# Causal mask of the transposed scores: from a TensorE matmul to GpSimd selects on the exponentials

## The reference

```python
q = (hidden_states @ q_w.T + q_b).reshape(b, s, H, HEAD_DIM)
k = hidden_states @ k_w.T + k_b
v = hidden_states @ v_w.T + v_b
scores = jnp.einsum('bqhd,bkd->bhqk', q, k) / HEAD_DIM ** 0.5
causal = jnp.triu(jnp.ones((s, s), dtype=bool), k=1)
scores = jnp.where(causal[None, None], -jnp.inf, scores)
attn = jax.nn.softmax(scores.astype(jnp.float32), axis=-1).astype(q.dtype)
out = jnp.einsum('bhqk,bkd->bqhd', attn, v).reshape(b, s, H * HEAD_DIM)
return out @ o_w.T + o_b
```

## Time and profile before

| | us |
|---|---|
| median of three runs | 2301.51 |
| lowest and highest | 2300.06, 2307.46 |
| span of the profiled execution | 2299.0 |
| TensorE busy in it | 2144.2 |
| VectorE busy | 1156.6 |
| ScalarE busy | 730.3 |
| GpSimd busy | 473.0 |

### The profile page before, as it was taken

The page is one execution under the profiler, slowest core; times in us unless marked ns, Lnnn a source line. Parts: engine busy times, 40 slices in busy tenths (PEclk is TensorE's granted clock), DMA queues, the critical chain, the costliest instruction groups (busy, mean ns, idle before and its releaser), DMA issues. The chain is left out here.

```text
span 2299.0 us, 33530 instructions
## 1 busy us (share of the span) xinstructions
PE 2144.2 (93%) x11910; PEld 1650.0 (72%) x11910; DVE 1156.6 (50%) x2233; ACT 730.3 (32%) x1273; POOL 473.0 (21%) x851
## 2 busy tenths in 40 slices
PE   6999999999999827999999999999999999999995
PEld 4666676666766516777777777778888888888884
DVE  4666857668576655444444444444424334334232
ACT  3434435344353322444333333332111111111111
POOL 2222414224142212111111111000120220220213
PEclk9999999999999956999999999999999999999998
DMA  6045141451413122444444444333120220210202
GB/s 170 30 108 146 60 131 52 116 140 63 132 49 101 56 74 93 149 148 154 158 158 164 169 161 147 131 110 114 38 91 18 73 91 18 73 61 31 90 19 92
DMA packets 106894, 228.78 MB, mean 100 GB/s; under 512 B 9664, under 2 KB 23744, under 8 KB 103648
## 3 DMA queue, kind: packets, MB, share of 16 engines
q1 hardware_dynamic: 94368, 187.28, 25.3%
q0 software_dynamic: 12480, 40.90, 5.9%
HBM read 160.52 MB, written 66.06 MB: 99 GB/s over the span
## 5 line engine op out<-in xcount | busy, mean ns | idle before, releaser
L1041 PE MATMUL ex_bank<-ex_xT,ex_gu 128*128 128x512 f32 (+1 forms) x1656 | 391.8, 395 | 1.5 <-DVE ex_xT L1075 1.5
L1041 PEld LDWEIGHTS ex_bank<-ex_xT,ex_gu 128*128 128x128 f32 (+1 forms) x1656 | 297.7, 180 | 87.8 <-issue 1.9
L1091 DVE TENSOR_TENSOR sh_silu<-sh_silu,sh_bank 128x512 f32<-128x512 f32 x88 | 60.5, 688 | 444.7 <-ACT sh_silu L1084 401.3
L740 ACT ACTIVATE at_PT<-at_bank 128x512 f32<-128x512 f32 (+1 forms) x384 | 187.4, 526 | 264.6 <-PE at_bank L446 258.3
L590 DVE TENSOR_REDUCE at_nmax<-at_bank 128x1 f32<-128x384 f32 (+3 forms) x512 | 216.7, 472 | 107.1 <-PE at_bank L394 107.1
L1041 PE MATMUL sh_bank<-sh_xT,sh_gate 128*128 128x512 f32 x1056 | 256.2, 392 | 4.1 <-DVE sh_xT L1075 4.1
L1053 PE MATMUL sh_bank<-sh_dn,sh_act 128*128 128x512 f32 x1056 | 255.2, 391 | 0.0
L1041 PE MATMUL sh_bank<-sh_xT,sh_up 128*128 128x512 f32 x1056 | 254.0, 389 | 0.0
L1084 ACT ACTIVATE sh_silu<-sh_bank 128x512 f32<-128x512 f32 x88 | 52.6, 598 | 586.6 <-PE sh_bank L1041 533.6
L800 POOL TENSOR_TENSOR at_minus_max<-idf,at_nmax 128x512 fp32r<-128x512 f32 x128 | 133.7, 1044 | 506.4 <-DVE at_nmax L590 488.0
L1041 PEld LDWEIGHTS sh_bank<-sh_xT,sh_gate 128*128 128x128 f32 x1056 | 199.7, 189 | 46.0 <-DVE sh_xT L1075 4.3
(11 more groups left out here) (207 smaller groups left out, 2882.0 us busy)
## 6 DMA issues: line engine op xcount, KB each, us to landing
ex_gu_in<-gu_in SPq DMA_DIRECT2D x23, 1408.0 KB
at_Qs<-q_dram SPq DMA_DIRECT2D x96, 256.0 KB, 5.8
ys<-sh_yk SPq DMA_DIRECT2D x23, 1024.0 KB, 5.8
q_dram<-at_q_h SPq DMA_DIRECT2D x64, 256.0 KB, 4.3
ex_dn_in<-dn_in SPq DMA_DIRECT2D x23, 512.0 KB
at_x_in<-x_in SPq DMA_DIRECT2D x8, 1024.0 KB, 10.1
at_x_res<-x_in SPq DMA_DIRECT2D x8, 1024.0 KB, 6.3
x<-at_y SPq DMA_DIRECT2D x8, 1024.0 KB, 8.1
```

The lines of the kernel that those rows point to most:

```text
L740: nc.scalar.activation(PT[g % 2][:, h % HG, TFROM[tb]:TFROM[tb] + TW[tb]], T_ps[tb][:, 0:TW[tb]], ACT.Exp).then_inc(pt_ready, 1)
L1041: last = self.nc.tensor.matmul(self.gate_up_ps[c % 2][which][0:m, :], cols(i, k), self.xT[j][:, k, :], start=(step == 0), stop=(step == 3 ...
L1091: nc.vector.tensor_tensor(silu[c % 2][0:m, :], silu[c % 2][0:m, :], gate_up_ps[c % 2][1][0:m, :], ALU.mult).then_inc(s["product"], 1)
```

## The change

The mask matmul of the transposed scores is removed, so that the exponentials of the diagonal blocks hold values for queries earlier than the key too. After the exponentials GpSimd replaces those by zero. A new function, drop_later_queries(b, h), waits for the three units of head h and runs two affine_select on PT in place: one over three of the diagonal blocks (at columns 0, 512 and 1024, evenly spaced), one over the fourth (at column 640). The second signals a new semaphore, pt_masked. Both products over keys now follow a wait for pt_masked in place of pt_ready.

```diff
@@ -413,7 +414,7 @@
                     if s in AV_STEP:
                         g = AV_STEP.index(s)
-                        pe.wait_ge(pt_ready, 3 * H * b + 3 * HG * (g + 1))
+                        pe.wait_ge(pt_masked, H * b + HG * (g + 1))
@@ -439,8 +440,6 @@
-                            nc.tensor.matmul(T_ps[tb][:, 0:len(tiles) * P], mask[:, 0, :],
-                                             idb[:, 0:len(tiles), :].rearrange("p t k -> p (t k)"), start=False, stop=False)
@@ -453,7 +452,7 @@
-                pe.wait_ge(pt_ready, 3 * H * b + 3 * H)
+                pe.wait_ge(pt_masked, H * b + H)
@@ -790,6 +789,18 @@
+            def drop_later_queries(b, h):
+
+                pool.wait_ge(pt_ready, 3 * h + 3)
+                pool.wait_ge(pt_ready, 3 * H * b + 3 * h + 3)
+                pt = PT[(h // HG) % 2][:, h % HG, :]
+                spread = pt.rearrange("p (t k) -> p t k", k=P)[:, 0:QT * QT // 2 + 1:QT, :]
+                nc.gpsimd.affine_select(out=spread, in_=spread, compare_op=ALU.is_ge, fill=0.0, base=0,
+                                        pattern=[[0, QT - 1], [1, P]], channel_multiplier=-1)
+                nc.gpsimd.affine_select(out=pt[:, TOFF[1]:TOFF[1] + P], in_=pt[:, TOFF[1]:TOFF[1] + P],
+                                        compare_op=ALU.is_ge, fill=0.0, base=0, pattern=[[1, P]],
+                                        channel_multiplier=-1).then_inc(pt_masked, 1)
@@ -800,12 +811,15 @@
+                    if h > 0:
+                        drop_later_queries(b, h - 1)
                     if h == 5 and not first:
                         norm[1].refine(b - 1)
                     if h == 8 and not last:
                         norm[0].refine(b + 1)
                     if 8 <= h < 8 + QT and not first:
                         add_residual(b - 1, h - 8)
+                drop_later_queries(b, H - 1)
```

More of the change, by code:

```diff
@@ L213, in build_attention @@
         x1_ready, diagonal_ready, made = sem("x1_ready"), sem("diagonal_ready"), sem("made")
+        pt_masked = sem("pt_masked")
         S_UNITS = [((2, 0), (0, (QT - 1) * P)), ((3, 0),), ((1, 0),)]
```

## The result

| | us, median (range) | runs |
|---|---|---|
| before | 2302.24 (2300.06 to 2307.46) | 4 |
| after | 2338.23 (2332.76 to 2339.73) | 4 |
| ratio after / before | 1.016 (95%: 1.0142 to 1.0178) | |

The changed kernel is slower by 36.0 us. The forecast was +17.5: the sign is right and the time lies in the range of 2290 to 2345, but the loss is twice what the sum gave. The profiled executions differ by 38.9 us of span (2337.9 against 2299.0), so they can be used to look for it.

A forecast was written before the change was run, and what follows sets the result against it. TensorE was taken as the bound, with the loop through VectorE's maxima and GpSimd's minus_max nearly closed. Span 2299.0 + 17.2 (6 x 2.4 + 0.3 + 2.5) + 2.5 around the span = 2319 us; range 2290 to 2345.

The forecast's parts named there:

- the sum: Attention stage: six steady turns at +2.4, first turn +0.3, last turn +2.5, together 17.2 us slower.
- T without a wait: Transposed part of a head's scores on TensorE: 1.70 us with three masks, 1.40 without, 0.30 saved a head.
- the MEMSET slope: Low bound for GpSimd's 384-column select: 0.8 ns a column, giving 0.49 us; 0.53 was taken.
- the residual add: High bound for the 384-column select: a two-input GpSimd operation, 1.275 us for 512 columns, so 0.96.
- the rival with the dear select: GpSimd's 384-column select goes at the two-input add's pace, a drop of 1.3 us: 22 us more, 2341; 8%.
- the three groups named: Groups 0 to 2, steps 5, 9, 13: TensorE's product over keys waits for selects, 1.3 to 1.7 us each.
- the fourth group's: Its product stands behind 60 products of the next sequence's projections, so its drop is hidden, except in the last turn.
- The gain lands in part only: Of 38 us gross, plain steps gain little: 0.6 by head 5's scores, then 0.3 for each of seven heads.
- the step-by-step working: Shifts through a steady turn: products of groups 0, 1, 2 at +0.7, +1.6, +3.0, turn's end at +2.4 us.
- at full granted clock: Reading of a steady turn before the change: TensorE busy 94.0 of 96.4 us at full clock.
- VectorE and GpSimd hold each other up: Rival: three hits of 0.5 us a turn on VectorE's path to the maxima add 12 us, 2331; 9%.
- 0.3 for the first turn: No residual adds and no chain at head 5 there: three waits against seven gains, about +0.3 us.

The follow-up runs named there:

- the kernel with the low halves later: The changed kernel with VectorE's low_mixed (L601) of groups 0 and 1 moved one step later: 2317.34 us, ratio 1.0064 to before.
- the filler: The changed kernel with five products of 512 columns, result overwritten, put on TensorE ahead of the wait for the selects: 2322.94 us, ratio 1.0094 to before.
- the control with the low halves later: The kernel before with low_mixed of groups 0 and 1 one step later and nothing else: 2301.81 us, ratio 1.0005.
- the kernel with masks and selects: The changed kernel with the mask matmuls kept, so the selects and the wait for them come on top: 2349.56 us, ratio 1.0183 to before.
- the changed kernel with the products a step later: The changed kernel with the products over keys of groups 0 to 2 moved from step 4g+5 to 4g+6: 2310.23 us, ratio 1.0037 to before.

## Why the prediction was right in kind and wrong in size

A steady turn's +6.09 us, taken apart along a row of neighbouring kernels (turn 3). In the first, the second and the last row the two kernels differ in one edit. The third and the fourth go through the kernel with the low halves later, and so differ in the place of L601 too (the fourth also in the filler, which costs nothing elsewhere in the turn); the split between these two rests on that:

| part | from | us |
|---|---|---|
| masks away, nothing in their place | 94.20 - 96.39 | -2.19 |
| 16 drops in GpSimd's queue, nobody waits for them | 95.62 - 94.20 | +1.42 |
| products wait for them, no hold-up | 98.30 - 95.62 | +2.68 |
| hold-up between VectorE and GpSimd | 99.13 - 98.30 | +0.83 |
| the halved clock, twice | 102.48 - 99.13 | +3.35 |

**What held.** T without a wait takes 1.39 us (358.05 to 359.44), forecast 1.40. The select of 384 columns takes 0.52, forecast 0.53, so the choice of the MEMSET slope over the residual add was right, and the rival with the dear select falls. The waits are in the three groups named, 25 in all and 38.6 us against 36, and the fourth group's is hidden in every turn but the last. The gain lands in part only, as forecast, and a little less than forecast (2.19, against 0.6 for heads up to 5 and seven times 0.3 for the rest). The first three rows of the table are what the step-by-step working covered; they make +1.91, and it had +2.4. With the low halves later, so without hold-up and at full clock, the products of groups 0, 1 and 2 start 0.55, 1.5 and 2.3 us later in the turn than in before, where it had 0.7, 1.6 and 3.0.

**Luck.** That 2338 lies inside the range is no merit of the working: its upper part stood there for a dear select, which did not come, and for a hold-up on VectorE's side. The halved clock had no place in it.

**The step that failed first: the sum had no term for TensorE's clock.** It is worth 3.35 of the +6.09. The text read "at full granted clock" off and took that for all of after. But the change puts idle time where there had been none, and a row that was shown already told what may come of it: in the earlier trace rows the product of 32 matmuls takes 3.89 us, in the earlier trace rows the same 32 take 2.36. Before that 3.89 TensorE had waited 1.40 us for minus_max and 0.60 for the exponentials (timeline of before, turn 7; the last row is the stretch with the granted clock):

```profile
773.11 0.50 PE L440 MATMUL at_bank<-at_Qs,at_Ks 96*128 96x512 f32 x1 [1.40 <-POOL at_minus_max L800]
...
775.00:785.00 10.00, 8.04 (x81) 4.16 (x82) 4.64 (x6) 4.68 (x9) 1.67 (x9) 0.83 0.28 106
```

I read of that row only its wait. 3.89 - 2.36 = 1.5 us was a measured price for what a new wait may bring behind it, and with waits of 1.3 to 1.7 us forecast in three places of each turn it belonged in the rivals with the largest price: up to 18 x 1.5 = 27 us. It came 9 times from turn 2 to turn 6 (twice a turn, once in the last of them): 9 x 1.67 = 15.0 us, and over turns 1 to 6 the filler gives back 15.1. Turn 0 has two more. Up to the scores of head 15 they make it 1.9 us longer than with the filler (60.8 against 58.9). Its whole length hides this (93.94 and 93.71), because the filler kernel has a halved stretch of its own at the end of turn 0, at the projection with wo. The same matmuls in before, then in the filler kernel, with its clock:

```profile
127.47 5.75 PE L481 MATMUL at_bank<-at_wo,at_OT 128*128 128x512 f32 x24 [1.44 <-DVE at_V L528]
...
127.37 7.38 PE L482 MATMUL at_bank<-at_wo,at_OT 128*128 128x512 f32 x24 [1.44 <-DVE at_V L529]
...
128.00:131.40 3.40, 3.40 (x10) 2.65 (x9) 0.42 (x1) 0.00 (x0) 0.00 (x0) 0.50 1.08 266
```

**The second: each select was priced alone.** It is worth 0.83 of the +6.09. The rival "VectorE and GpSimd hold each other up" had 9% and 12 us, and looked for the hit on VectorE's side, at L110, in front of the maxima. It came at L798 on GpSimd's side, where TensorE waits directly: 0.5 us on the wait of group 1 and 0.45 on that of group 2. The neighbour, L601, stands in VectorE's queue behind the maxima of each step 4g+8, next to the very drop that the product of the next group needs; to see that, one has to lay VectorE's queue beside GpSimd's new one, and I had laid only GpSimd's. The Trainium skill (SBUF — State Buffer, SBUF: two separate sides) names just this pair: a VectorE operation with two SBUF inputs against a GpSimd operation that reads SBUF, exclusive for the whole instruction. This case's rows agree: 0.52 beside the maxima, which read PSUM, 1.04 and 0.97 beside L601.

A row already shown had the sign of it on GpSimd's side. In the earlier trace rows the first operation of the chain behind head 8 takes 0.57, where the last one of the chain before takes 0.20; it starts beside low_mixed, which is L602 in before. In the control with the low halves later it takes 0.20, and another one of the chain takes 0.52, beside L602's new place (before, then the control):

```profile
360.10 0.68 DVE L602 TENSOR_TENSOR at_OT<-at_mixed_f,at_OT 128x512 fp32r<-128x512 f32 x1
...
359.14 0.20 POOL L123 TENSOR_TENSOR at_t_x<-at_t_x 128x4 f32<-128x4 f32 x1
...
360.57 0.71 DVE L602 TENSOR_TENSOR at_OT<-at_mixed_f,at_OT 128x512 fp32r<-128x512 f32 x1
360.82 0.52 POOL L123 TENSOR_TENSOR at_t_x<-norm_constants,at_t_x 128x4 f32<-128x4 f32 x1
```

Both kernels take the same time: here nobody waits for that operation.

With the low halves moved, most halved stretches are gone too, which makes 21 us for both; that the shorter waits are what spared them is my reading of it, and not separately shown.

**The turns.** The forecast had 0.3 for the first turn (measured +3.7, of which 1.9 is the clock, as above; its waits for the selects are 0.77, 1.85 and 0.90 us, and why so little of them came back is not taken apart), 14.4 for turns 1 to 6 (measured +31.8), and 2.5 for turn 7 (with all behind it, +5.2).

**What stays open.** When a wait brings a halved stretch I cannot say from these runs. In turn 1 of after the same two waits stand as in turn 3, 1.93 and 1.83 us, and both products run in 2.36:

```profile
170.90 2.36 PE L372 MATMUL at_bank<-at_PT,at_ones_f 128*32 128x512 f32 x32 [1.93 <-POOL at_PT L800]
187.62 2.36 PE L372 MATMUL at_bank<-at_PT,at_ones_f 128*32 128x512 f32 x32 [1.83 <-POOL at_PT L800]
```

That is why turn 1 costs +2.9 and turn 3 +6.1: with the filler both cost the same (98.13 - 95.35 = 2.8, 99.13 - 96.39 = 2.7). In turns 1 to 6 of after the wait of 1.93 brought one in 5 of 6, that of 1.83 in 4 of 6, that of 1.16 never. In the kernel with masks and selects a wait of 1.60 brought a halved stretch in each of turns 2 to 6 but not in turn 1, and one of 1.51 none; in turn 2 of the kernel with the low halves later a wait of 1.41 brought one, in turn 3 an equal one none. The wait of 2.05 for minus_max in the changed kernel with the products a step later brought one in two of five turns. And the wait of 1.44 at the end of turn 0 brought none in before and one in before with the low halves later. So within after the longer waits did it more often, but the length of one wait doesn't decide by itself, and a forecast can only give it a share: here 9 of the 18 waits of turns 1 to 6.

## What to carry to other kernels

A new wait on a dense TensorE can cost more than its own length: look in the trace of before for the same group of matmuls at two durations, take the difference as a price, and carry it as a rival behind every wait that the change adds (in the steady turns here half of the waits of 1.16 to 1.93 us brought it). Work moved to an idle engine was cheap here as long as TensorE did not wait for its results (1.42 us a turn); give that engine only the pieces whose results are wanted late, and leave the last piece before each consumer where it was. Where VectorE and GpSimd both read SBUF, lay their two queues side by side at the places where a third engine waits, and try moving the neighbour by one step before giving the change up.

## What the runs showed of the hardware

- The granted clock of TensorE fell to one half (1.2 of 2.4 GHz) in stretches of 3.4 us behind 9 of the 18 new waits (1.16 to 1.93 us) of turns 1 to 6, inside otherwise dense work, each costing some 1.67 us; with five matmuls put into the wait it stayed at 1.00 in these turns.
- An affine_select in place takes 0.52 us for 384 columns of 128 partitions in float32 and 0.29 for 128; beside a VectorE operation with two SBUF inputs (L601, 0.68 us) the former took 0.97 and 1.04, and with that operation a step later none of the 128 took more than 0.525.
- A mask matmul of 128 or 256 bf16 columns between larger products costs TensorE about 0.10 us of its pace (T 1.39 against 1.70 with three of them), half of the 0.232 that its own row shows as busy.
